# One projection of q and k per group and 32-row feature products in an attention and expert kernel

## The chip, the cores and the metric

The kernel runs on one core of one Trainium2 chip. The core has a matrix engine (TensorE, PE in the profile; PEld is its loading of weights), a vector engine (VectorE, DVE), a scalar engine (ScalarE, ACT), a general engine (GpSimd, POOL) and a queue that issues transfers (SyncE, SP). The engines run side by side, each in the order of its own program, and meet only at semaphores. SBUF is the working memory with 128 partitions, PSUM the memory of eight banks into which TensorE writes. The metric is the device time of one execution in microseconds (us); lower is better.

## The reference, cut to what matters

```
h   = layernorm(x) * (1 + ca) + sa               # x: (4, 1024, 128)
q, k, v = split(h @ w_qkv.T, 3)                  # 8 heads of 16, blocks of 32 tokens
qp  = elu(einsum('bhcsd,hdf->bhcsf', q, proj)) + 1.0     # 128 features
kp  = elu(einsum('bhcsd,hdf->bhcsf', k, proj)) + 1.0
kv  = einsum('bhcsf,bhcsd->bhcfd', kp, v)
num = einsum('bhcsf,bhcfd->bhcsd', qp, kv)
z   = 1.0 / (einsum('bhcsf,bhcf->bhcs', qp, kp.sum(axis=3)) + 1e-08)
x   = x + ga * ((num * z) @ w_out.T + b_out)
h   = layernorm(x) * (1 + cb) + sb
x   = x + gb * expert_ffn(h)                     # one of 8 experts per token, 128 -> 512 -> 128
```

elu(y) + 1 is y + 1 for positive y and exp(y) for the rest.

## The kernel before, in words

The 4096 tokens are 32 tiles of 128. Four tiles are a group, so there are 8 groups, and each group is worked through in 8 head steps (`step(g, ...)` on each engine, with `for h in range(H)` in it). After the last group come the expert slots: tokens are written to a table in device memory sorted by expert, and 39 tiles of 128 rows are read back, multiplied by the weights of their expert and written out. This tail is not touched by the change.

One head step needs the features of q and of k. The weights of projection and features are multiplied together once at the start (`fold`, L755, into `mix_hi` and `mix_lo`, split in two parts so that products in the rounded float32 form keep their precision), and `feats(g, h)` (L810 to L812) makes for each of q and k (index `j`) three products of 128x128 weights with 512 columns of the normalised, transposed input `hT`, which is also split (`hT_hi` by DVE at L1074, `hT_lo` by POOL at L424). They land in two banks, `x_ps[h % 2]`; there are two such pairs. ACT takes relu(-y) of both banks (L577) and then exp of its negative in two halves (L581); DVE makes max(y, 0) plus that, in two halves (`features`, L1179), into `phi`. TensorE then multiplies the features within blocks of 32 tokens (`scores`, L821, 16 small products), ACT copies the result (L588), and once per four heads `apply_values` (L835) multiplies it with the values. The values stand in `vbd`, spread so that each block of 32 tokens sees its own only: DVE writes them with four masked products per group (`keep_values`, L1187).

The order on each engine is written out by hand. Per head step TensorE runs `feats(g, h)`, then for some h one block of other work, then `scores` of the head two before: `values` (L852) at h = 0, `gate` (L864) at h = 3, `project_out` (L843) at h = 5, `rank` (L870) at h = 7; `apply_values` follows at h = 0 and 2, `turn_h2` (L858) at h = 2 and `turn_xn` (L763) at h = 5, each behind the scores. A pair of banks is free for head h + 2 when DVE has made the features of head h. DVE puts the pieces of the norms, the normalising, the routing and the residual of earlier groups between its `features`.

Of the kernel before, what the change touches and what calls it, by code (L numbers as in the profile page):

```python
# [19 lines left out]
P = 128  # L20
ALU = mybir.AluOpType
ACT = mybir.ActivationFunctionType
AX = mybir.AxisListType
F32 = mybir.dt.float32
# [4 lines left out]
EPS = 1e-5  # L29


def adaln_kernel(nc, x, w_qkv, w_out, b_out, proj, w_red, wg, w1, b1_t, w2, b2, c_cols, wmod, out):
# [37 lines left out]
    with ctx:  # L70
# [9 lines left out]
        proj_bd = sb("proj_bd", [P, H, FEAT])  # L80
        mix_hi = sb("mix_hi", [P, 2, H, FEAT], F32R)
        mix_lo = sb("mix_lo", [P, 2, H, FEAT], F32R)
# [10 lines left out]
        silu_bc = sb("silu_bc", [P, B, P])  # L93
# [16 lines left out]
        blk_mask = sb("blk_mask", [P, NC, VW])  # L110
# [10 lines left out]
        zeros = sb("zeros", [P, 4 * D])  # L121
# [4 lines left out]
        hT_hi = sb("hT_hi", [P, 2, GT], F32R)  # L126
        hT_lo = sb("hT_lo", [P, 2, GT], F32R)
        vals = sb("vals", [P, TG, H, HD])
# [3 lines left out]
        vbd = sb("vbd", [P, TG, H, NC, VW])  # L132
        den = sb("den", [P, TG * NC])
        rden = sb("rden", [P, TG * NC])
        o_sb = sb("o_sb", [P, TG * NC, 2, HD])
        oT = sb("oT", [P, TG, P])
# [79 lines left out]
        w_slot.append(proj_bd[:, :, :].rearrange("p h f -> p (h f)")[:, 0:F + D])  # L216
# [3 lines left out]
        yo_early = vbd[:, :, :, :, :].rearrange("p t h c w -> p (t h c w)")[:, 0:EARLY * D].rearrange("p (s d) -> p s d", d=D)  # L220
# [22 lines left out]


        l_attn = sem("l_attn"); l_mod = sem("l_mod"); l_c = sem("l_c"); l_gate = sem("l_gate"); l_x0 = sem("l_x0"); l_x = sem("l_x")
        l_exp = sem("l_exp")
        c_pool = sem("c_pool"); c_tri = sem("c_tri"); c_dve = sem("c_dve"); c_exp = sem("c_exp"); set_silu = sem("set_silu")
        p_mix = sem("p_mix"); p_cols = sem("p_cols"); p_wv = sem("p_wv"); p_rows = sem("p_rows"); p_turn = sem("p_turn"); p_gate = sem("p_gate")
        set_khi = sem("set_khi"); set_mix = sem("set_mix"); set_cols = sem("set_cols"); set_wv = sem("set_wv"); set_rows = sem("set_rows")
# [5 lines left out]
        s_neg = sem("s_neg"); s_xb = sem("s_xb"); s_gbs = sem("s_gbs"); s_scat = [sem(f"s_scat{i}") for i in range(RECS)]  # L255
        s_phi = sem("s_phi"); s_ln1 = sem("s_ln1"); s_xn = sem("s_xn"); s_vbd = sem("s_vbd"); s_nrm = sem("s_nrm")
# [12 lines left out]
        def _(sp):  # L269
            sp.dma_start(wqkv_sb[:, :, :], w_qkv.rearrange("(j r) d -> r j d", j=3)).then_inc(l_attn, 16)  # L270
            sp.dma_start(proj_bd[:, 0, :], proj.rearrange("h k f -> (h k) f")).then_inc(l_attn, 16)
            xt = xf.rearrange("(t p) d -> p t d", p=P)
            sp.dma_start(x_all[:, 0:TG, :], xt[:, 0:TG, :]).then_inc(l_x0, 16)
            sp.dma_start(cT[:, :], c_cols).then_inc(l_c, 16)
            sp.dma_start(wmod_sb[:, :], wmod).then_inc(l_mod, 16)
            sp.dma_start(wo_sb[:, :], w_out).then_inc(l_gate, 16)
# [3 lines left out]
            sp.dma_start(x_all[:, TG:NT, :], xt[:, TG:NT, :]).then_inc(l_x, 16)  # L280
            by_expert = w1b2[:, :].rearrange("p (e f) -> p e f", e=E)
            sp.dma_start(by_expert[:, :, 0:F], w1.rearrange("e d f -> d e f")).then_inc(l_exp, 16)
            sp.dma_start(w2_sb[:, :].rearrange("p (e c d) -> p e c d", e=E, c=FC),
                         w2.rearrange("e (c p) d -> p e c d", p=P)).then_inc(l_exp, 16)
            sp.dma_start(b1_cols[:, :], b1_t).then_inc(l_exp, 16)
            sp.dma_start(by_expert[:, :, F:F + D], b2.rearrange("(a e) f -> a e f", a=1).partition_broadcast(P)).then_inc(l_exp, 16)

            sp.wait_ge(c_dve, 1)
            for e in range(E + 1):
                sp.dma_start(sorted_rows[e * REGION:e * REGION + P, :], pad_rec[:, :]).then_inc(s_tail, 16)  # L290
# [1357 lines left out]
```

## Time and profile before

| | us |
|---|---|
| median of 3 runs | 293.17 |
| lowest, highest | 292.45, 293.57 |
| span of the profiled execution | 292.5 |
| TensorE busy | 264.7 |
| VectorE busy | 233.8 |
| ScalarE busy | 224.2 |
| GpSimd busy | 166.2 |

The span has three parts: the start up to the first feature product at 11.87 us, the eight groups up to 185.5 us, and the expert tail. All groups from the third to the seventh have the same length within 0.2 us, so one of them stands for five. A busy share of TensorE is not a measure of what it has left, because products overlap; the distance between the starts of two products is. For a chain of engines that wait for each other one looks at what ends last before each product.

### The profile page before, as it was taken

What the parts mean: (1) busy time and instruction counts of PE and PEld (TensorE: products, weight loads), DVE (VectorE), ACT (ScalarE), POOL (GpSimd) and SP (SyncE); (2) the same over time, 40 slices, a digit from 0 to 9 for tenths busy, and PEclk for the clock granted to TensorE, in tenths of its full rate; (3) what the DMA queues carried; (4) which work ended last, traced back from release to release, by engine and by line L of the source; (5) the groups of instructions that cost most, each with busy time, mean ns of one, the idle gap of its engine ahead of it and who ended that gap; (6) DMA issues with size and microseconds to landing.
All of it is one profiled execution on the core that took longest, in us unless ns stands there. A gap on an engine that the chain in (4) does not pass through costs nothing.

```text
span 292.5 us, 11379 instructions
## 1 busy us (share of the span) xinstructions
PE 264.7 (91%) x3952; PEld 212.3 (73%) x3953; DVE 233.8 (80%) x772; ACT 224.2 (77%) x516; POOL 166.2 (57%) x193
## 2 busy tenths in 40 slices
PE   8999799999999999999999999899686999999970
PEld 2566576678778777777777776678575999999960
DVE  3787969989999999999999989988884476676750
ACT  2589698999989989989989988856964667676740
POOL 7004154344476675675685681878788874454551
PEclk9999999999999999999999999999999999999996
DMA  5999800000001001001001011513355344444400
GB/s 149 286 358 300 199 3 2 2 4 4 2 29 56 30 29 56 31 29 57 29 29 56 29 45 70 163 58 113 126 168 176 117 126 123 112 126 131 117 28 0
DMA packets 16239, 26.13 MB, mean 89 GB/s; under 512 B 2608, under 2 KB 11060, under 8 KB 16193
## 3 DMA queue, kind: packets, MB, share of 16 engines
q1 hardware_dynamic: 12896, 17.10, 21.2%
q0 software_dynamic: 3296, 8.41, 8.0%
q8 instruction: 30, 0.49, 0.8%
q14 instruction: 17, 0.13, 0.2%
HBM read 15.32 MB, written 10.64 MB: 89 GB/s over the span
## 4 chain that ended last, share of the span: by engine, by line
PE 45%; DVE 20%; issue 8%; ACT 8%; POOL 5%; DMA 2%; POOLq 1%; ACTq 0%; DVEq 0%; SPq 0%
PE ps L885 9%; DVE phi L1179 8%; PE ps L913 8%; PE ps L810 6%; PE ps L812 4%; PE ps L811 4%; PE ps L821 3%; ACT ebuf L577 3%; ACT ebuf L581 2%; PE ps L843 2%; POOL sorted_rows L458 2%; DVE h L1248 2%; PE ps L835 2%; DVE ln_st L1231 2%; PE ps L879 1%
## 5 line engine op out<-in xcount | busy, mean ns | idle before, releaser
L1179 DVE SCALAR_TENSOR_TENSOR phi<-ps,ebuf 128x512 f32<-128x512 f32 x128 | 81.9, 680 | 13.2 <-ACT ebuf L581 13.1
L577 ACT ACTIVATE ebuf<-ps 128x1024 f32<-128x1024 f32 x64 | 65.5, 1024 | 15.5 <-PE ps L812 15.0
L581 ACT ACTIVATE ebuf<-ebuf 128x512 f32<-128x512 f32 x128 | 74.4, 636 | 0.1
L810 PE MATMUL ps<-hT_hi,mix_lo 128*128 128x512 f32 x128 | 58.4, 456 | 8.1 <-DVE phi L1179 4.5
L635 ACT ACTIVATE gT<-ps,b_cols 128x128 f32<-128x128 f32 x156 | 44.6, 367 | 17.1 <-PE ps L885 14.6
L812 PE MATMUL ps<-hT_hi,mix_hi 128*128 128x512 f32 x128 | 50.6, 396 | 0.0
L811 PE MATMUL ps<-hT_lo,mix_hi 128*128 128x512 f32 x128 | 50.6, 395 | 0.0
L913 PE MATMUL ps<-w_sb,gT 128*128 x312 | 42.3, 278 | 4.0 <-DVE y L1501 2.8
L913 PEld LDWEIGHTS ps<-w_sb,gT 128*128 128x128 f32 x312 | 37.9, 192 | 6.0 <-issue 5.9
L527 POOL DMA_INDIRECT out<-yo,tok x27 | 27.0, 1001 | 23.8 <-DVE yo L1517 21.9
L458 POOL DMA_INDIRECT sorted_rows<-rec,pos x32 | 32.6, 1017 | 8.4 <-issue 6.6
L810 PEld LDWEIGHTS ps<-hT_hi,mix_lo 128*128 128x128 f32 x128 | 24.0, 187 | 17.1 <-DVE phi L1179 6.2
L821 PEld LDWEIGHTS ps<-phi 128*32 128x32 f32 x2048 | 22.2, 112 | 15.7 <-issue 11.7
L377 POOL TENSOR_TENSOR ln_rs<-ln_ve,neg_half 128x4 f32<-128x4 f32 x16 | 16.7, 1045 | 26.6 <-DVE ln_ve L1067 23.7
L821 PE MATMUL ps<-phi 128*32 128x32 f32 x2048 | 29.3, 199 | 0.0
L812 PEld LDWEIGHTS ps<-hT_hi,mix_hi 128*128 128x128 f32 x128 | 24.0, 188 | 5.8
L424 POOL TENSOR_TENSOR hT_lo<-hT,hT_hi 128x512 fp32r<-128x512 f32 x7 | 8.9, 1277 | 34.0 <-DVE hT_hi L1074 34.0
L811 PEld LDWEIGHTS ps<-hT_lo,mix_hi 128*128 128x128 f32 x128 | 24.1, 189 | 3.7 <-issue 1.0
L885 PE MATMUL ps<-sT,x_all 128*128 128x128 f32 x184 | 25.0, 279 | 0.3 <-ACT sT L626 0.3
L885 PEld LDWEIGHTS ps<-sT,x_all 128*128 128x128 f32 x184 | 22.3, 191 | 0.8 <-issue 0.4
L588 ACT COPY a_sb<-ps 128x128 f32<-128x128 f32 x64 | 16.9, 265 | 5.0 <-PE ps L821 5.0
L1488 DVE COPY x_all<-w1b 128x640 f32 x19 | 9.8, 516 | 10.4 <-issue 10.4
(208 smaller groups left out, 465.2 us busy)
## 6 DMA issues: line engine op xcount, KB each, us to landing
rin<-sorted_rows SPq DMA_DIRECT2D x39, 192.5 KB, 2.5
w1b<-in_L_ffn_w SPq DMA_DIRECT2D x1, 2048.0 KB, 14.2
sorted_rows<-pad_rec SPq DMA_DIRECT2D x9, 192.5 KB, 6.2
w1b<-in_L_ffn_b SPq DMA_DIRECT2D x1, 512.0 KB, 7.4
sorted_rows<-rec,pos POOLq DMA_INDIRECT x32, 3.1
out<-yo,tok POOLq DMA_INDIRECT x27
wmod_sb<-in_L_wmod SPq DMA_DIRECT2D x1, 384.0 KB, 4.0
x_all<-in_L_attn_x SPq DMA_DIRECT2D x1, 256.0 KB, 3.4
```

The costliest lines, as they stand in the source:

```text
L458: g_.indirect_dma_start(out=sorted_rows[:, :], out_offset=bass.IndirectOffsetOnAxis(ap=pos[:, g % RECS, t:t + 1], axis=0), in_=rec[:, g % ...
L527: g_.indirect_dma_start(out=of[:, :], out_offset=bass.IndirectOffsetOnAxis(ap=tok[:, b:b + 1], axis=0), in_=yo[:, b, :], in_offset=None, b ...
L577: nc.scalar.activation(ebuf[:, h % 2, :, :], x_ps[h % 2], ACT.Relu, scale=-1.0).then_inc(s_neg, 1)
L581: nc.scalar.activation(ebuf[:, h % 2, j, :], ebuf[:, h % 2, j, :], ACT.Exp, scale=-1.0).then_inc(s_exp, 1)
L635: last = nc.scalar.activation(gT[:, b, c_, :], h_ps[b][:, j, i * P:(i + 1) * P], ACT.Gelu, bias=b1_cols[:, bass.ds(e * FC + c_, 1)])
L810: mm(x_ps[h % 2][:, j, :], mix_lo[:, j, h, :], hi, start=True, stop=False)
L811: mm(x_ps[h % 2][:, j, :], mix_hi[:, j, h, :], lo, start=False, stop=False)
L812: mm(x_ps[h % 2][:, j, :], mix_hi[:, j, h, :], hi, start=False, stop=True).then_inc(s_x, 1)
L821: last = mm(a_ps[c_ * BLK:(c_ + 1) * BLK, t * BLK:(t + 1) * BLK], phi[:, h % 4, 1, at:at + BLK], phi[:, h % 4, 0, at:at + BLK], start=True ...
L885: last = mm(h_ps[b % 2][:, j, i * P:(i + 1) * P], w[:, c_ * P:(c_ + 1) * P], sT[:, b % 2, :], start=True, stop=True)
L913: last = mm(y_bank(early, b), gT[:, b % 2, c_, :], w2_sb[:, bass.ds(e * (FC * D) + c_ * D, D)], start=(c_ == 0), stop=(c_ == FC - 1))
L1179: v.scalar_tensor_tensor(out=phi[:, h % 4, j, :], in0=x_ps[h % 2][:, j, :], scalar=0.0, in1=ebuf[:, h % 2, j, :], op0=ALU.max, op1=ALU.add ...
```

## The change

Projection of q and k. The fold is gone. Once a group, `project(g, j)` multiplies the 128x128 weights `wqkT` of q and of k (plain float32) with 512 columns of `hT`. ACT copies the result to `qk` in the rounded form (`keep_hi`), DVE subtracts that from the product to get the second part (`split_lo`). This is done a group ahead: `turn_xn(g + 1)` at h = 0, `project` at h = 1 and h = 4, `values(g + 1)` at h = 7. `hT_hi`, `hT_lo` and their instructions on DVE and POOL are gone.

Features. A head's feature product now contracts over 32 rows: `proj_w` holds the feature weights of two heads in each 32 rows, with the rows of the other head zero. q uses the rows of group h // 2, k the rows two groups further, so that the two lie in different quarters of the array's rows. There are three products for each of q and k, in turns of q and k, and then one more for each, of a constant `unit` with a broadcast of itself, which adds one (scaled). Everything is scaled by `SHRINK`, 2 to the power of -39.

Clamp. ACT makes one exp of both banks, straight from PSUM. DVE makes min(exp, SHRINK) and the max of that with the product, for both banks in one instruction. `keep_a` undoes the scale.

Values. ACT writes the values with a column of ones in `vals`, and SP copies them with four transfers per group to the diagonal of `vbd`, which is zeroed once. The masked products on DVE and the mask are gone.

Besides: the additions of epsilon behind both norms' moments go from DVE to POOL; the first norm runs two groups ahead; x is loaded first; loads of the expert weights are spread over groups 1 to 4 instead of standing at the start; the feature weights are loaded by ACT's queue and built on POOL (`make_proj`); the index tables are made later.

```
-            def fold(j, i):
-                mm(ps[:, 2 * i + j, :], wqkv_sb[:, j, :], proj_bd[:, 4 * i:4 * i + 4, :].rearrange("p h f -> p (h f)"),
-                   start=True, stop=True).then_inc(p_mix, 1)
+            def project(g, j):
+                if j == 0:
+                    pe.wait_ge(s_ht, g + 1)
+                elif g:
+                    pe.wait_ge(s_lo, 2 * g + 1)
+                if g == 0:
+                    pe.wait_ge(set_w, 1)
+                mm(k_first if g == 0 and j == 1 else t_ps, wqkT[:, j, :], hT[:, :], start=True, stop=True).then_inc(s_qk, 1)
...
             def feats(g, h):
                 if h == 0:
-                    pe.wait_ge(s_lo, g + 1)
...
+                    pe.wait_ge(s_lo, 2 * g + 2)
...
+                if not (g == 0 and h < 2):
+                    pe.wait_ge(s_phi, H * g + h - 1)
+                at = (h // 2 * BLK, (h // 2 + 2) % NC * BLK)
+                for w_part, part in ((0, 1), (1, 0), (0, 0)):
+                    for j in range(2):
+                        rows = slice(at[j], at[j] + BLK)
+                        mm(x_ps[h % 2][:, j, :], proj_w[rows, w_part, j, h % 2, :], qk_of(g, part, j)[rows, :],
+                           start=w_part < part, stop=False)
                 for j in range(2):
-                    if not (isinstance(g, int) and g == 0 and h < 2):
-                        pe.wait_ge(s_phi, 2 * (H * g + h) - 3 + j)
-
-                    mm(x_ps[h % 2][:, j, :], mix_lo[:, j, h, :], hi, start=True, stop=False)
-                    mm(x_ps[h % 2][:, j, :], mix_hi[:, j, h, :], lo, start=False, stop=False)
-                    mm(x_ps[h % 2][:, j, :], mix_hi[:, j, h, :], hi, start=False, stop=True).then_inc(s_x, 1)
+                    rows = slice(at[j], at[j] + BLK)
+                    last = mm(x_ps[h % 2][:, j, :], unit[rows, :], unit[rows, 0:1].broadcast_to([BLK, GT]), start=False, stop=True)
+                last.then_inc(s_x, 1)
...
-                nc.scalar.activation(ebuf[:, h % 2, :, :], x_ps[h % 2], ACT.Relu, scale=-1.0).then_inc(s_neg, 1)
-                between()
-                act.wait_ge(s_neg, H * g + h + 1)
-                for j in range(2):
-                    nc.scalar.activation(ebuf[:, h % 2, j, :], ebuf[:, h % 2, j, :], ACT.Exp, scale=-1.0).then_inc(s_exp, 1)
+                nc.scalar.activation(ebuf[:, h % 2, :, :], x_ps[h % 2], ACT.Exp, scale=1.0 / SHRINK,
+                                     bias=math.log(SHRINK) - 1.0).then_inc(s_exp, 1)
+
+            def keep_hi(g, j):
+                act.wait_ge(s_qk, 2 * g + j + 1)
+                from_ps = k_first if isinstance(g, int) and g == 0 and j == 1 else t_ps
+                nc.scalar.copy(qk_of(g, 0, j), from_ps).then_inc(s_hi, 1)
...
-                for j in range(2):
-                    dve.wait_ge(s_exp, 2 * (H * g + h) + j + 1)
-                    v.scalar_tensor_tensor(out=phi[:, h % 4, j, :], in0=x_ps[h % 2][:, j, :], scalar=0.0,
-                                           in1=ebuf[:, h % 2, j, :], op0=ALU.max, op1=ALU.add).then_inc(s_phi, 1)
-
-            def keep_values(g, c, first):
-                dve.wait_ge(s_vs, g + 1)
...
-                last = v.tensor_scalar(vbd[:, :, :, c, 0:HD].rearrange("p t h d -> p (t h) d"),
...
+                dve.wait_ge(s_exp, H * g + h + 1)
+                v.scalar_tensor_tensor(out=phi[:, h % 4, :, :], in0=ebuf[:, h % 2, :, :], scalar=SHRINK,
+                                       in1=x_ps[h % 2], op0=ALU.min, op1=ALU.max).then_inc(s_phi, 1)
...
+            def split_lo(g, j):
+                dve.wait_ge(s_hi, 2 * g + j + 1)
+                from_ps = k_first if g == 0 and j == 1 else t_ps
+                v.tensor_tensor(qk_of(g, 1, j), from_ps, qk_of(g, 0, j).bitcast(F32), ALU.subtract).then_inc(s_lo, 1)
...
+            def spread_values(g):
+                sp.wait_ge(s_vs, g + 1)
+                if g == 0:
+                    sp.wait_ge(c_vbd, 2)
+                else:
+                    sp.wait_ge(s_av, 2 * g)
+                for c in range(NC):
+                    sp.dma_start(vbd[c * BLK:(c + 1) * BLK, c, :],
+                                 vals[c * BLK:(c + 1) * BLK, :, :, :].rearrange("p t h w -> p (t h w)")).then_inc(s_vbd, 16)
```

TensorE in a middle group, around the border to the next group. Before: the last products of head 0, then the values, the scores of an earlier head and the first half of the apply.

```order
L810 MATMUL ps<-hT_hi,mix_lo 128x512
L811 MATMUL ps<-hT_lo,mix_hi 128x512
L812 MATMUL ps<-hT_hi,mix_hi 128x512
L852 MATMUL ps<-wvT,hT 128x128 x4
L821 MATMUL ps<-phi 32x32 x16
L835 MATMUL ps<-vbd,a_sb 32x68 x16
L810 MATMUL ps<-hT_hi,mix_lo 128x512
```

After, from the values of the next group to the scores behind the projection (`qk,proj_w` and `unit` are the feature products, `hT,wqkT` the projection).

```order
L905 MATMUL ps<-wvT,hT 128x128 x4
L862 MATMUL ps<-qk,proj_w 128x512 x6
L866 MATMUL ps<-unit 128x512 x2
L815 MATMUL ps<-ident,xn 128x128 x4
L876 MATMUL ps<-phi 32x32 x16
L890 MATMUL ps<-vbd,a_sb 32x68 x16
L862 MATMUL ps<-qk,proj_w 128x512 x6
L866 MATMUL ps<-unit 128x512 x2
L826 MATMUL ps<-hT,wqkT 128x512
L876 MATMUL ps<-phi 32x32 x16
```

The values have moved ahead of head 0, the transpose of xn from h = 5 to h = 0, and the projection stands between a head's feature products and the scores.

VectorE in a middle group, heads 2 to 5. Before, with the masked products L1187 and the rounding L1074:

```order
L1219 STREAM_TRANSPOSE oT<-o_sb 128x512
L1179 SCALAR_TENSOR_TENSOR phi<-ps,ebuf 128x512 x2
L1187 TENSOR_SCALAR vbd<-vals,blk_mask 128x32x16 x2
L1179 SCALAR_TENSOR_TENSOR phi<-ps,ebuf 128x512 x2
L1266 TENSOR_REDUCE top<-lg_sb 128x4
L1187 TENSOR_SCALAR vbd<-vals,blk_mask 128x32x16
L1271 TENSOR_TENSOR lgd<-lg_sb,top 128x32
L1187 TENSOR_SCALAR vbd<-vals,blk_mask 128x32x16
L1276 SCALAR_TENSOR_TENSOR cand<-lgd,rev 128x32
```

After, heads 1 to 4; `qk<-ps,qk` is `split_lo`, here of q (that of k stands behind head 5):

```order
L1230 SCALAR_TENSOR_TENSOR phi<-ebuf,ps 128x1024 x2
L1134 TENSOR_TENSOR qk<-ps,qk 128x512
L1238 TENSOR_SCALAR den<-ps 128x16
L1127 BN_AGGR ln_mv<-ln_st 128x2 x4
L1242 RECIPROCAL rden<-den 128x16
L1246 TENSOR_TENSOR o_sb<-ps,rden 128x16x16
L1254 STREAM_TRANSPOSE oT<-o_sb 128x512
L1230 SCALAR_TENSOR_TENSOR phi<-ebuf,ps 128x1024 x2
L1300 TENSOR_REDUCE top<-lg_sb 128x4
```

Four masked products and the small epsilon instruction are gone between the features, and the split stands at head 2 in front of the normalising.

## Rows read from the trace of the kernel before

**Rows 1.** The page: the chain that ended last, by engine.

```profile
PE 45%; DVE 20%; issue 8%; ACT 8%; POOL 5%; DMA 2%; POOLq 1%; ACTq 0%; DVEq 0%; SPq 0%
```

**Rows 2.** Busy time by stretch; third, fifth and last group; columns in the first line.

```profile
core 0: us, PE busy (x) PEld busy (x) DVE busy (x) ACT busy (x) POOL busy (x), PEclk, DMA share, GB/s
55.46:77.10 21.64, 21.18 (x406) 16.50 (x407) 19.24 (x59) 19.74 (x40) 8.95 (x8) 1.00 0.01 3
...
98.54:120.17 21.63, 20.92 (x406) 16.37 (x406) 20.12 (x64) 19.60 (x38) 14.36 (x14) 1.00 0.11 39
...
163.38:185.50 22.12, 20.57 (x401) 15.88 (x402) 20.58 (x66) 18.92 (x37) 12.52 (x14) 1.00 0.16 55
```

**Rows 3.** TensorE in order of time, one head: start, us, engine, line, idle before.

```profile
89.79 0.40 PE L812 MATMUL ps<-hT_hi,mix_hi 128*128 128x512 f32 x1
90.12 0.46 PE L821 MATMUL ps<-phi 128*32 128x32 f32 x32
90.51 0.50 PE L810 MATMUL ps<-hT_hi,mix_lo 128*128 128x512 f32 x1
90.84 0.40 PE L811 MATMUL ps<-hT_lo,mix_hi 128*128 128x512 f32 x1
91.07 0.40 PE L812 MATMUL ps<-hT_hi,mix_hi 128*128 128x512 f32 x1
...
91.78 0.40 PE L812 MATMUL ps<-hT_hi,mix_hi 128*128 128x512 f32 x1
92.01 1.05 PE L843 MATMUL ps<-wo_g,oT 128*128 128x128 f32 x8
```

**Rows 4.** TensorE in order of time, values, scores, apply, next head.

```profile
100.04 1.05 PE L852 MATMUL ps<-wvT,hT 128*128 128x128 f32 x8
...
101.30 0.70 PE L835 MATMUL ps<-vbd,a_sb 128*32 128x68 f32 x32
...
101.93 0.49 PE L810 MATMUL ps<-hT_hi,mix_lo 128*128 128x512 f32 x1
...
102.04 0.19 PEld L811 LDWEIGHTS ps<-hT_lo,mix_hi 128*128 128x128 f32 x1
...
102.26 0.40 PE L811 MATMUL ps<-hT_lo,mix_hi 128*128 128x512 f32 x1
```

**Rows 5.** In order of time at the start: weight loads of a plain float32 product.

```profile
7.19 0.19 PEld L755 LDWEIGHTS ps<-proj_bd,wqkv_sb 128*128 128x128 f32 x1 [0.51 <-issue]
...
7.62 0.19 PEld L755 LDWEIGHTS ps<-proj_bd,wqkv_sb 128*128 128x128 f32 x1 [0.24 <-issue]
```

**Rows 6.** Groups by line, 76.95 to 98.54 us: busy, mean ns, idle before and releaser.

```profile
L1179 DVE SCALAR_TENSOR_TENSOR phi<-ps,ebuf 128x512 f32<-128x512 f32 x17 | 10.9, 679 | 1.2 <-ACT ebuf L581 1.2
L1187 DVE TENSOR_SCALAR vbd<-vals,blk_mask 128x512 f32<-128x512 f32 x4 | 2.4, 627 | 0.0
...
L1241 DVE TENSOR_SCALAR ln_ve<-ln_mv 128x4 f32<-128x4 f32 x1 | 0.8, 799 | 0.0
...
L581 ACT ACTIVATE ebuf<-ebuf 128x512 f32<-128x512 f32 x16 | 9.3, 636 | 0.0
L577 ACT ACTIVATE ebuf<-ps 128x1024 f32<-128x1024 f32 x9 | 9.2, 1024 | 1.4 <-PE ps L812 1.3
```

**Rows 7.** VectorE in order of time, one head's features and what follows.

```profile
81.82 1.27 DVE L1179 SCALAR_TENSOR_TENSOR phi<-ps,ebuf 128x512 f32<-128x512 f32 x2
83.02 0.16 DVE L1203 TENSOR_SCALAR den<-ps 128x16 f32<-128x16 f32 x1
```

**Rows 8.** Start, in order of time: hT, its rounding, its second part, first product.

```profile
9.85 0.78 ACT L597 ACTIVATE hT<-ps,modT 128x512 f32<-128x512 f32 x1 [0.59 <-PE ps L763]
10.66 0.43 DVE L1074 CAST hT_hi<-hT 128x512 fp32r<-128x512 f32 x1 [0.21 <-ACT hT L597]
11.13 0.69 DVE L1106 TENSOR_TENSOR hT_lo<-hT,hT_hi 128x512 fp32r<-128x512 f32 x1
11.87 0.50 PE L810 MATMUL ps<-hT_hi,mix_lo 128*128 128x512 f32 x1 [0.23 <-DVE hT_lo L1106]
```

More of the change, by code:

```diff
@@ L513, in _ @@
             step(2, nxt=True, prev=True, prev2=True, firstp2=True)
-            for g in range(3, NG - 1):
-                step(g, nxt=True, prev=True, prev2=True, prev3=True)
-            step(NG - 1, prev=True, prev2=True, prev3=True)
+            for g in range(3, NG):
+                step(g, nxt=g + 2 < NG, prev=True, prev2=True, prev3=True)
             def put_early(s):
@@ L745, in keep_busy, with turn_xn @@
                     mm(bank, ones_b[:, :], ones_b[:, :].unsqueeze(1).broadcast_to([P, 4, P]), start=True, stop=True)
-            pe.wait_ge(c_pool, 2)
+            pe.wait_ge(c_ones, 1)
             keep_busy(11, m_ps)
-            pe.wait_ge(c_pool, 10)
-            pe.wait_ge(l_attn, 32)
-            def fold(j, i):
-                mm(ps[:, 2 * i + j, :], wqkv_sb[:, j, :], proj_bd[:, 4 * i:4 * i + 4, :].rearrange("p h f -> p (h f)"),
-                   start=True, stop=True).then_inc(p_mix, 1)
-            def turn_xn(g, first):
+            pe.wait_ge(c_ident, 2)
+            pe.wait_ge(l_attn, 16)
+            for j in range(3):
+                last = nc.tensor.transpose(ps[:, j, 0:P], wqkv_sb[:, j, :], ident[:, :])
+            last.then_inc(p_w, 1)
+            pe.wait_ge(set_silu, 1)
+            pe.wait_ge(l_mod, 16)
+            for j in range(2):
+                last = mm(ps[:, 3, 8 * j:8 * j + B], wmod_sb[:, j * D:(j + 1) * D], siluT[:, :], start=True, stop=True)
+            last.then_inc(p_cols, 1)
+            def turn_xn(g):
                 pe.wait_ge(s_xn, g + 1)
-                if not first:
+                if g:
                     pe.wait_ge(s_vs, g)
@@ L796, in setup_gate @@
             def setup_gate():
                 pe.wait_ge(set_turn, 1)
-                mm(ps[:, 6, 0:E], wredT[:, :], wgT[:, :], start=True, stop=True).then_inc(p_gate, 1)
+                mm(m_ps[:, 0:E], wredT[:, :], wgT[:, :], start=True, stop=True).then_inc(p_gate, 1)
             def feats(g, h):
                 if h == 0:
-                    pe.wait_ge(s_lo, g + 1)
-                if isinstance(g, int) and g == 0 and h < 2:
-                    pe.wait_ge(set_mix, h + 1)
-                hi, lo = (part[:, bass.ds(g % 2, 1), :].rearrange("p a n -> p (a n)") for part in (hT_hi, hT_lo))
@@ L831, in apply_values @@
                     pe.wait_ge(s_on, 2 * g + half)
-                to = o_ps_last if is_last(g) and half == 1 else o_ps
+                to = o_of(g, half)
                 for t in range(TG):
@@ L961, in step @@
                         apply_values(g - 1, 1, False)
-                    if h == 5 and nxt:
-                        turn_xn(g + 1, False)
-            step(0, False, False, True)
-            step(1, True, False, True)
-            for g in range(2, NG - 1):
-                step(g, True, True, True)
-            step(NG - 1, True, True, False)
+                    if h == 7 and nxt:
+                        values(g + 1)
+            turn_xn(0)
+            project(0, 0)
+            project(0, 1)
+            values(0)
+            for g in range(NG):
+                step(g, g >= 1, g >= 2, g + 1 < NG)
             pe.wait_ge(s_vs, NG)
@@ L1474, in step @@
                         if prev2:
[L1475 to L1482 removed]
+                            position_out(g - 2)
+            for g in range(NG):
+                step(g, g >= 1, g >= 2, g + 1 < NG, g + 2 < NG, firstp=g == 1, firstp2=g == 2)
             def take_weights(s, b):
```

456 lines of the change are left out of this document (225 added, 231 removed).

## The prediction

> **What bounds the kernel now.** I read the chain first: TensorE holds 45% of it and VectorE 20% [rows 1]. Then the busy time by stretch: in a middle group of 21.63 us TensorE is busy 20.92, VectorE 20.12 and ScalarE 19.60, all at a granted clock of 1.00, that is the 2.4 GHz level [rows 2]. Three engines are nearly full, so the distances between starts must tell which one sets the length. In one head the scores start 0.39 us ahead of the next head's feature products, and these take from 90.51 to 92.01 when a full-width block follows, that is 1.50 us for six [rows 3]. Inside, one product follows the other after 0.23 us (90.84 to 91.07), but the step into the feature products is 0.33 (90.51 to 90.84) and the step from their last product to the scores is 0.33 as well (89.79 to 90.12): 0.10 us more wherever TensorE changes between full and quarter-width tiles [rows 3]. So a head costs 1.60 + 0.39 = 1.99 us, eight of them 15.9 us, and the rest of the 21.6 is mostly the blocks of 128x128 products (the values alone, eight passes, about 1.0 [rows 4]). TensorE has hardly any slack; any engine that is relieved beside it gives nothing by itself.
>
> **The change part by part, for a middle group.** I keep p for the time that one pair of new feature products (q and k) takes on TensorE.
>
> Feature products: six of 0.235 us and two changes of 0.10 are replaced by four pairs and the same two changes. If q and k run side by side in their different rows, p is 0.235, the duration of one. If they don't, p is 0.47. The trace of before has no product of 32 rows. The nearest row is the apply, with tiles that differ in columns: 32 products of 68 columns between 101.30 and 101.93, 0.020 us each [rows 4], where a plain float32 pass over 512 columns takes 0.43 us [rows 5], so 68 columns would take 0.057 us one after the other. 2.9 of four tiles run at once there. With two tiles I take full overlap, p = 0.235, and keep 0.47 as the other end. A head then costs 4 x 0.235 + 0.19 = 1.13 us in place of 1.60; 8 x 0.47 = 3.8 us saved.
>
> The Trainium skill, in TensorEngine Tiling (Key Properties), says the same: tiles work independently and can load weights and multiply in parallel. TensorE: Matmul & The Clock Gate (Measured speedup vs the span model) gives 3.07 times for four row tiles; an estimate from that page's figure would put two tiles between 1.5 and 2 times, p = 0.235 to 0.31.
>
> Projection: two plain float32 products of 512 columns, two passes each. Their weight loads stand 0.43 us apart [rows 5], so 4 x 0.43 = 1.7 us added.
>
> Tile changes: feature products were full width, so nothing was lost when values, gate, output projection or rank followed directly (91.78 to 92.01 is 0.23 [rows 3]). Now each block of full-width work next to them costs one change more: the transpose of xn, two projections, gate, output projection, rank and values, 7 x 0.10 = 0.7 us. TensorEngine Tiling (Key Properties) speaks against the change here: it says that switching the tiling mode drains TensorE. By that rule, the trace agrees, and the 0.10 us is the price; without it the sum would be 0.7 us a group better.
>
> The group in total is 21.6 - 12.8 + 8 x (4p + 0.19) + 2.4 = 12.7 + 32p. At p = 0.235 this is 20.2 us, a gain of 1.3 to 1.4; it is zero at p = 0.278. The margin is thin: 0.04 us a pair.
>
> ScalarE: the two exps (16 in 9.3 us) go, relu becomes exp on the same 1024 elements (1.02 us [rows 6]), and two copies of 512 columns come, about 0.6 each by the size of the exp rows. 19.6 - 9.3 + 1.2 = 11.5 us: far from the bound.
>
> VectorE: four masked products (2.4 us), the epsilon instruction (0.8) and the rounding (0.43) go [rows 6, 8]; two splits of 0.69 come [rows 8]; the one 1024-wide feature instruction costs as much as the two did or a little less (81.82 to 83.02, 1.20 us [rows 7]). 20.1 - 3.6 + 1.4 - 0 to 0.5 = 17.4 to 17.9 us. That fits into 20.2 with some two us to spare. This relief is what lets TensorE have its gain; without it VectorE's 20.1 would be as late as TensorE.
>
> GpSimd loses `hT_lo` and gets two tiny additions; it is at 14.4 of 21.6 [rows 2]. Its wait for `hT_hi` stood in front of a scatter and of the next norm; now both norms start with a wait for VectorE's moments, and behind it in GpSimd's queue stand a scatter and the scale of a record, which nobody needs before the following group. Cost nothing. The values by transfer: SP waits for the apply at h = 2 of a group, the reader is the apply at h = 0 of the next, some 15 us later. Four transfers cost nothing unless the queue is held for longer than that; the loads of expert weights are issued behind them, in groups 1 to 4, with the next spread a group later, and nothing on SP is urgent until the last group. The prologue's padding writes move past the spread for group 1, hidden too.
>
> **Start.** Before, hT starts at 9.85 and the first product at 11.87 [rows 8]. x comes one issue earlier, but VectorE now scales the turned weights ahead of the modulation columns; I leave hT's end at 10.6. Then projection 0.86, copy 0.6, split 0.69, and about 0.6 more because the k half follows through the same two engines: first feature product near 13.4, +1.5 us. The ends are +0.5 (the earlier x counts fully) and +3.
>
> **Sum over the groups.** Group 0: VectorE and the modulation rows bind it; it loses the masked products and gets splits, I take -2.0 (0 to -3). Group 1 has no gate, rank or turn of h2 and waited for features more; -1.5. Groups 2 to 6: 5 x -1.3 = -6.5; the ends are -2, if new waits cost 0.9 us a group, and -10, if the tile changes cost nothing more than today. Group 7, 22.12 us [rows 2]: no projection, no transpose, no values behind it, and VectorE, at 20.58 the later engine there, loses 3.2 us; -3.0 (-1 to -4). Tail: the same instructions, 0. Sum: +1.5 - 2.0 - 1.5 - 6.5 - 3.0 = -11.5 us. 292.5 - 11.5 = 281.0 for the profiled execution; the median of before is 0.7 above its span, so 281.7 us. With all ends of the small terms the forecast's own range is 274 to 290.
>
> **Rivals.**
> 1. No overlap of q and k: p = 0.47. Against it speaks the apply; for it, that this row is of column tiles and of another form of number. It adds 32 x 0.235 = 7.5 us a group, 60 us in all: 342 us. This is the case on the other side, and it decides from p = 0.278 on.
> 2. Weight loads in the same rows wait. Head by head the next pair uses the same rows, and if a load there had to wait for the product in flight, p would be 0.235 plus a load, at most 0.13 (eight loads and passes of the values in 1.05 us [rows 4]). Against it: the load at 102.04 starts while the product of 101.93 runs over all rows, and the next product follows at 102.26 [rows 4]. It would add 32 x 0.13 = 4.2 us a group: 315 us. TensorE: Matmul & The Clock Gate (The mechanism) states that loads overlap a running product only when the row groups differ; by that rule this case would hold, and the trace disagrees for full-width loads. A milder form of 1 or 2, p near 0.3, gives 281.7 + 8 x 2.1 = 298.
> 3. The gain turns into a wait on VectorE. Features are now given and freed whole, not in halves: products 1.13, exp 1.02, features 1.2 and three hand-overs make about 3.7 us for a pair of banks, against 5.0 in two heads. That leaves 1.3 us; heads 6, 7, 0 and 2 carry most of VectorE's other work, and where a head is later than that TensorE waits. If this takes the whole gain of the middle groups: 281.7 + 6.5 = 288, up to 292.
> 4. Something not in the views (a granted clock that falls to 1.2 GHz, transfers that come late): 5%, mostly slower.
>
> **How the numbers follow.** Forecast 0.66, rival 1 0.09, rival 2 with its milder form 0.10 (half each), rival 3 0.10, rival 4 0.05. The range must leave out no more than 0.2: it starts at 273, below the forecast's own, and goes to 300 to take in rival 3 and the milder form; 315 and 342 stay out. About 0.5% (1.5 us) is what a measurement can tell from no change. Faster: nearly all of the forecast and two thirds of rival 3, 0.73. Same: the last third and a little, 0.06. Slower: 0.21.
>
> **What would show it.** Right: the starts of feature products in pairs within some ten ns, pairs 0.235 us apart; middle groups of 20.2 us; ScalarE busy near 12 us a group; no wait of the apply for `vbd`; first feature product near 13.4. Wrong: starts 0.23 us apart one by one (rival 1); pairs at 0.36 (rival 2); TensorE idle ahead of feature products and released by VectorE for over 1 us a group (rival 3).

## The result and the profile after

The changed kernel takes 305.27 us (median of 4 runs, 300.59 to 316.24), the kernel before 293.37 us in the same sitting (median of 4, 292.45 to 293.76). The ratio is 1.0295 with a 95% interval of 1.0222 to 1.0368: slower by 3%, where 281.7 us and a gain of 4% were forecast, and outside the range of 273 to 300. The ratio rests on the two faster runs, 300.59 and 303.59 us; the profiled execution took 306.96 us, with a span of 304.9 and a mean granted clock of 0.892. The four clocks are 0.911, 0.891, 0.892 and 0.845, in the order of the times: 300.59, 303.59, 306.96, 316.24.

The times follow the clocks, except that the middle two clocks are equal. The page of the profile has the granted clock in tenths, in 40 slices. Before (slices of 7.3 us):

```profile
PEclk9999999999999999999999999999999999999996
```

After (slices of 7.6 us), with the busy share of TensorE above it:

```profile
PE   7599799999999999999999989999778799999970
PEclk9689979996559999996559998799999799999996
```

TensorE stays busy and the clock falls all the same. The next view gives, for stretches of 3 us, busy time and count of each engine (PE, PEld, DVE, ACT, POOL), then the granted clock, the share of the DMA engines and GB/s:

```profile
69.00:72.00 3.00, 3.00 (x53) 2.04 (x49) 2.93 (x11) 1.38 (x3) 1.72 (x3) 0.93 0.41 93
72.00:75.00 3.00, 3.00 (x38) 1.43 (x38) 2.19 (x6) 1.35 (x3) 1.60 (x2) 0.50 0.86 271
93.00:96.00 3.00, 3.00 (x78) 1.80 (x76) 1.22 (x1) 2.29 (x4) 1.08 (x2) 1.00 0.18 68
141.00:144.00 3.00, 3.00 (x40) 1.68 (x40) 2.08 (x6) 0.87 (x3) 2.53 (x3) 0.50 0.11 42
```

A clock of 0.50 is the 1.2 GHz level. TensorE has no idle time in any of the four, and in the two slow ones it gets half as many instructions done (38 and 40 against 78). Nor is it idle ahead of a long fall: in every stretch from 54 to 180 us it is busy for 3.00 of 3.00 us, and in that time the clock falls twice, near 71.5 and near 139.8 us, for some 20 us each. Two shorter falls, near 41 and near 188 us, come close behind or in a stretch with idle time. (The ends of products are modelled in the trace, so very short gaps would not show; before_rows32, below, doesn't rest on this.) The transfers are no common sign: a share of 0.86 in one, 0.11 in the other.

Group by group, from one hT activation (L645) to another, the same view:

```profile
62.87:90.61 27.74, 27.74 (x426) 18.62 (x420) 19.05 (x53) 13.15 (x23) 11.70 (x14) 0.66 0.27 72
90.61:111.21 20.60, 20.60 (x445) 14.28 (x437) 16.55 (x47) 13.06 (x23) 10.98 (x13) 0.97 0.35 106
111.21:131.01 19.80, 19.80 (x435) 13.63 (x425) 17.77 (x52) 13.07 (x24) 13.55 (x16) 1.00 0.35 110
131.01:158.80 27.79, 27.79 (x431) 18.80 (x425) 19.49 (x56) 13.15 (x24) 16.61 (x19) 0.66 0.13 40
```

The group at a clock of 1.00 takes 19.80 us, where a middle group of before took 21.6 [rows 2] and 20.2 were forecast. The two groups at 0.66 take 27.7 and 27.8 us, each 7.9 to 8.0 more than the undisturbed one. So the change does in TensorE's program what the sum said, and the clock takes it back.

One head of the undisturbed group, and one at half clock (start, duration, engine, line; TensorE alone):

```profile
111.29 0.97 PE L862 MATMUL ps<-qk,proj_w 32*128 32x512 f32 x6
112.10 0.38 PE L866 MATMUL ps<-unit 32*128 32x512 f32 x2
112.41 1.13 PE L826 MATMUL ps<-hT,wqkT 128*128 128x512 f32 x2
```

```profile
81.72 1.64 PE L862 MATMUL ps<-qk,proj_w 32*128 32x512 f32 x6
83.17 0.62 PE L866 MATMUL ps<-unit 32*128 32x512 f32 x2
83.72 0.21 PE L923 MATMUL ps<-pick,before 128*128 128x40 bf16 x1
```

At the full clock eight products stand in 111.29 to 112.41, 1.12 us; before, six took 1.50 without the second change of tiles [rows 3]. At half clock they take 81.72 to 83.72, 2.00 us.

ScalarE and VectorE in the undisturbed group (engine, operation, count, busy time and mean ns, then the idle time before them and what ended it), to set beside [rows 6, 7]:

```profile
L622 ACT ACTIVATE ebuf<-ps 128x1024 f32<-128x1024 f32 x8 | 8.2, 1026 | 4.3 <-PE ps L866 4.3
L1230 DVE SCALAR_TENSOR_TENSOR phi<-ebuf,ps 128x1024 f32<-128x1024 f32 x8 | 9.7, 1209 | 1.8 <-ACT ebuf L622 1.8
L1134 DVE TENSOR_TENSOR qk<-ps,qk 128x512 fp32r<-128x512 f32 x2 | 1.4, 684 | 0.0
```

What idle time they have goes back to TensorE: ScalarE waits for its products, VectorE for ScalarE.

The start has a second miss. The rows that answer to [rows 8]:

```profile
7.29 1.03 POOL L437 TENSOR_TENSOR stage<-stage,half_mask 128x512 f32<-128x512 f32 x1
7.33 3.34 DVE L1148 TENSOR_SCALAR xn<-x_all,ln_mv,ln_rs 128x128 f32<-128x128 f32 x4
9.07 1.26 POOL L442 TENSOR_TENSOR proj_w<-stage,proj_w 128x512 fp32r<-128x512 f32 x1
10.73 1.12 PE L815 MATMUL ps<-ident,xn 128*128 128x128 f32 x4 [2.36 <-DVE xn L1148]
11.88 0.78 ACT L645 ACTIVATE hT<-ps,modT 128x512 f32<-128x512 f32 x1 [5.13 <-PE ps L815]
12.71 3.78 PE L826 MATMUL ps<-hT,wqkT 128*128 128x512 f32 x4 [0.87 <-ACT hT L645]
17.90 0.50 PE L862 MATMUL ps<-qk,proj_w 32*128 32x512 f32 x2 [0.20 <-DVE qk L1134]
```

The first feature product starts at 17.90, forecast 13.4, before 11.87. VectorE's four xn instructions take 3.34 us while GpSimd builds the feature weights (before, 1.11), and the projection of q and k takes 3.78 us at a granted clock of 0.50.

### The profile page after: what moved, and what is told of

The parts are those of the page before. It is cut to its first block, busy times and chain, and to the rows that moved or that the text cites. A ratio compares the mean times of both kernels' runs of the same rounds, so it can differ in the third digit from the quotient of the medians.

```text
span 304.9 us, 11533 instructions
## 1 busy us (share of the span) xinstructions
PE 277.7 (91%) x4106; PEld 207.1 (68%) x4107; DVE 217.8 (71%) x668; ACT 168.6 (55%) x400; POOL 160.7 (53%) x201
## 4 chain that ended last, share of the span: by engine, by line
PE 65%; DVE 8%; issue 5%; POOL 5%; DMA 2%; ACT 1%; POOLq 0%; DVEq 0%; SPq 0%
PE ps L862 17%; PE ps L938 9%; PE ps L966 8%; PE ps L876 7%; PE ps L826 4%; PE ps L866 4%; PE ps L898 3%; PE ps L905 3%; DVE phi L1230 3%; PE ps L890 3%; POOL sorted_rows L509 2%; PE ps L917 2%; PE ps L815 2%; DMA sorted_rows<-rec,pos 2%; PE ps L932 1%
## 5 line engine op out<-in xcount | busy, mean ns | idle before, releaser
L1230 DVE SCALAR_TENSOR_TENSOR phi<-ebuf,ps 128x1024 f32<-128x1024 f32 x64 | 77.5, 1211 | 36.0 <-ACT ebuf L622 36.0
L862 PE MATMUL ps<-qk,proj_w 32*128 32x512 f32 x384 | 69.5, 470 | 3.4 <-DVE phi L1230 3.2
L862 PEld LDWEIGHTS ps<-qk,proj_w 32*128 32x128 f32 x384 | 35.1, 208 | 15.1 <-DVE phi L1230 3.9
L876 PEld LDWEIGHTS ps<-phi 128*32 128x32 f32 x2048 | 24.6, 120 | 24.2 <-issue 16.2
L574 POOL DMA_INDIRECT out<-yo,tok x27 | 27.1, 1003 | 25.1 <-DVE yo L1538 24.4
L876 PE MATMUL ps<-phi 128*32 128x32 f32 x2048 | 32.1, 208 | 0.2 <-issue 0.2
L636 ACT ACTIVATE a_sb<-ps 128x128 f32<-128x128 f32 x64 | 17.6, 275 | 21.5 <-PE ps L876 21.5
L866 PE MATMUL ps<-unit 32*128 32x512 f32 x128 | 26.8, 415 | 0.0
L826 PE MATMUL ps<-hT,wqkT 128*128 128x512 f32 x32 | 21.4, 764 | 0.9 <-ACT hT L645 0.9
L866 PEld LDWEIGHTS ps<-unit 32*128 32x128 f32 x128 | 13.4, 205 | 3.6
L676 ACT COPY sT<-ps 128x128 f32<-128x128 f32 x39 | 10.4, 266 | 8.9 <-PE ps L932 7.7
```

The lines of the kernel that those rows point to most:

```text
L574: g_.indirect_dma_start(out=of[:, :], out_offset=bass.IndirectOffsetOnAxis(ap=tok[:, b:b + 1], axis=0), in_=yo[:, b, :], in_offset=None, b ...
L636: nc.scalar.activation(a_sb[:, h // HH, h % HH, :, :], a_ps.rearrange("p (t s) -> p t s", t=TG), ACT.Copy, scale=SHRINK ** -2).then_inc(s_ ...
L826: mm(k_first if g == 0 and j == 1 else t_ps, wqkT[:, j, :], hT[:, :], start=True, stop=True).then_inc(s_qk, 1)
L862: mm(x_ps[h % 2][:, j, :], proj_w[rows, w_part, j, h % 2, :], qk_of(g, part, j)[rows, :], start=w_part < part, stop=False)
L866: last = mm(x_ps[h % 2][:, j, :], unit[rows, :], unit[rows, 0:1].broadcast_to([BLK, GT]), start=False, stop=True)
L876: last = mm(a_ps[c_ * BLK:(c_ + 1) * BLK, t * BLK:(t + 1) * BLK], phi[:, h % 4, 1, at:at + BLK], phi[:, h % 4, 0, at:at + BLK], start=True ...
```

## The experiments

The theory after the result: **rows at work**. The granted clock falls because the products of the features use 32 + 32 of the array's 128 rows at a time, though TensorE is never idle. The rivals: idle time and waits of TensorE, the bursts of transfers, or the other parts of the change (the shorter ScalarE and VectorE work, the values by transfer).

**rows64: the same program with 64 rows in each product.** q uses one half of the rows and k the other, in the same eight weight loads and eight products a head. In the six products with `proj_w` the weights of the other three heads in those rows are zero, so that the rows with weights that are not zero are as few as in the changed kernel; the two with `unit` have 64 such rows in place of 32.

```
-                at = (h // 2 * BLK, (h // 2 + 2) % NC * BLK)
+                at = (h // 4 * 64, (1 - h // 4) * 64)
...
-                        rows = slice(at[j], at[j] + BLK)
-                        mm(x_ps[h % 2][:, j, :], proj_w[rows, w_part, j, h % 2, :], qk_of(g, part, j)[rows, :],
+                        rows = slice(at[j], at[j] + 64)
+                        mm(x_ps[h % 2][:, j, :], proj_w[rows, w_part, j, h % 4, :], qk_of(g, part, j)[rows, :],
```

> The changed kernel with one thing altered: q and k feature products contract over 64 rows each (q in one half of the array's rows, k in the other), with the weight rows of the other heads zero, in place of 32. Same number of instructions and columns, the full computation. Theory A (the granted clock falls because the 32-row products keep too few of the array's rows at work): the clock stays at 0.97 or above, middle groups of about 20 us, 279 to 285 us. Theory B (the clock falls because of the order and the waits of the new program, whatever the rows): clock near 0.89 as in the changed kernel, 299 to 307 us.

Measured: 290.06 us (287.11 to 291.87, 4 runs, clocks 0.962 to 0.968), ratio to before 0.9855 (0.979 to 0.992). Two groups of it, and its row of the clock:

```profile
63.85:83.75 19.90, 19.90 (x435) 13.73 (x425) 17.27 (x48) 13.07 (x24) 9.04 (x11) 1.00 0.38 105
103.56:123.36 19.80, 19.80 (x435) 13.66 (x425) 17.77 (x52) 13.06 (x24) 13.58 (x16) 1.00 0.36 110
PEclk9669999999999999999999999999998899999996
```

The first of these is the group that took 27.74 us at 0.66 in the changed kernel; the second has the same 19.8 us, 435 products, load of transfers and relief of ScalarE as the undisturbed group there, and the clock is 1.00 in both. All that differs in the groups is how many rows a product uses. That takes out the rivals for the groups, and turns 305 into 290 us, 1.5% below before. Rows whose weights are zero count here as rows in use, in six of the eight products. Nor is it the chip: on one and the same chip proj_late, the changed kernel with one wait more, has a clock of 0.902 and rows64_late 0.976 to 0.981 (both below).

The time itself was missed: 279 to 285 us were expected by this theory, 299 to 307 by its rival, and 290 lies between. The first feature product comes at 20.25 us in place of 17.90, because GpSimd has twice as many weights to build; the clock is low there as well. The runs for the start, below, take this up.

**rows128: all 128 rows for each product**, so that q and k can't run side by side. Each product then contracts over all rows with the same weights, and so mixes four heads: the selection of the head is left out.

```
-                at = (h // 2 * BLK, (h // 2 + 2) % NC * BLK)
+                at = (0, 0)
...
-                        rows = slice(at[j], at[j] + BLK)
+                        rows = slice(0, P)
```

> The changed kernel with feature products over all 128 rows for q and for k (it sums over all heads, so the features are not those of the reference). A pair can no longer run side by side: both theories expect pairs at 0.47 us in place of 0.235, groups of about 27.5 us and 330 to 342 us if the clock is whole. Theory A: granted clock 0.98 or above in the groups. Theory B: it still falls in some groups, below 0.93, and the time is over 345.

Measured: 327.99 us (2 runs, clocks 0.968 and 0.981), ratio 1.1197 (1.1169 to 1.1226), just below the 330 to 342 us expected.

```profile
96.81:122.67 25.86, 25.86 (x435) 20.01 (x425) 18.08 (x50) 12.94 (x25) 14.00 (x16) 1.00 0.28 84
100.15 1.67 PE L862 MATMUL ps<-qk,proj_w 128*128 128x512 f32 x6
101.66 0.60 PE L866 MATMUL ps<-unit 128*128 128x512 f32 x2
102.19 0.46 PE L876 MATMUL ps<-phi 128*32 128x32 f32 x32
```

Eight products now need 100.15 to 102.19, 2.04 us, in place of 1.12. A group is 6.06 us longer. So q and k do run side by side in the changed kernel, and what that is worth is 6 us a group; rival 1's price was about right (7.5 us, less 0.7 for the seven tile changes that this kernel doesn't have), its condition false. A group of 27.5 us was expected and is 25.86; the clock in it is 1.00, as the theory says.

**before_rows32: the kernel before, with its feature products over the first 32 rows only** (the other 96 rows of the contraction are left out). Nothing of the change is in it.

```
-                    mm(x_ps[h % 2][:, j, :], mix_lo[:, j, h, :], hi, start=True, stop=False)
+                    mm(x_ps[h % 2][:, j, :], mix_lo[0:32, j, h, :], hi[0:32, :], start=True, stop=False)
...
```

> The kernel before, its order and its waits untouched, with the three feature products of each of q and k contracting over the first 32 rows only (part of the contraction is left out). A product takes as long whatever its rows. Theory A: the granted clock falls below 0.95 in the groups and the time rises to 298 or more. Theory B: clock 0.99 and 293 us as before.

Measured: 400.28 us (398.71 to 404.49, clocks 0.659 to 0.671), ratio 1.3647 (1.3589 to 1.3706).

```profile
134.00:171.60 37.60, 37.60 (x407) 27.22 (x407) 20.00 (x63) 19.95 (x37) 14.31 (x14) 0.50 0.06 23
PEclk9995655555555555555555555555589998999997
```

The theory expected a clock below 0.95 and 298 us or more. A group of 21.6 us becomes one of 37.6 by using fewer rows in the same products. TensorE is busy in all of it. This is the strongest run of the study: a kernel that had the full clock in all groups loses it with no other edit.

**before_rows64 and before_rows96** repeat it with 64 and 96 rows (the other 64 or 32 rows are left out); the slices read `[0:64]` and `[0:96]`.

> The kernel before with the three feature products of q and of k contracting over the first 64 rows only (part of the contraction is left out), order and waits untouched. Before: clock 0.99, 293 us; the same with 32 rows: clock 0.66, 400 us. Theory A in its strict form (what counts is the number of rows at work at a time, so that one product of 64 rows is like a pair of 32): clock between, falling in part of the groups, 0.85 to 0.95 and 298 to 325 us. If only tiles of 32 rows are at fault: clock 0.99 and 293 us.

> The kernel before with its feature products over the first 96 rows in place of 128 (rows 96 to 127 of the contraction are left out; instructions, columns and order are the same). Theory (the granted clock goes by how many rows of the array are at work): between the whole clock of before (0.99, 293 us) and that of 64 rows (0.83 and 0.73, 339 and 378 us); with a steep edge it may be whole: clock 0.93 to 0.99, 293 to 312 us. Rival (anything less than the full 128 rows loses it): clock at or under 0.83, 339 us or more.

Measured: with 64 rows 338.62 and 377.83 us, at clocks of 0.828 and 0.726; with 96 rows 294.32 us (292.05 to 296.3, clocks 0.971 to 0.987), ratio 1.0059 (1.0001 to 1.0117).

```profile
PEclk9999795557555555599977999969998999999996
80.00:100.00 20.00, 20.00 (x211) 14.15 (x210) 11.90 (x34) 11.66 (x23) 5.46 (x6) 0.53 0.01 2
```

These lines are of the kernel with 64 rows. In that with 96 only two slices are below 9, apart from the last, which is 6 before too:

```profile
PEclk9999889999999999999999999999999999999996
```

With 96 rows the run is as expected (0.93 to 0.99, 293 to 312 us). With 64 rows both runs lie outside what was expected (0.85 to 0.95, 298 to 325 us), and they differ by 39 us, so neither is the figure for 64 rows; the faster one, at 338.62, is far above before all the same. So the clock rises with the rows in this kernel: 0.66, 0.73 and 0.83, 0.97 to 0.99. It is also not a matter of 32-row products alone. The changed kernel has 64 rows at work too and a clock of 0.89, between 64 and 96 rows here. It has them for a smaller part of the time (1.1 of 2.5 us a head, where before_rows64 has 1.5 of 2.7 [rows 3]); that this makes the difference isn't shown.

**busy1: more work of full width.** One bf16 product of 128 rows and 512 columns goes ahead of each head's features, into a bank that the features overwrite.

```
+                if True:
+                    keep_busy(1, x_ps[h % 2][:, 0, :])
```

> The changed kernel plus one bf16 product of 128 rows and 512 columns ahead of each head's feature products, into the bank that these overwrite (64 in all, about 0.235 us each at the 2.4 GHz level, 15 us). Theory A: the granted clock stays at 0.97 or above, and 281.7 + 15 = 295 to 299 us. Theory B: clock near 0.89 and 312 us or more.

Measured: 304.88 us (300.62 to 305.83, clocks 0.953 to 0.969), ratio 1.0324 (1.025 to 1.0398). The clock rises from 0.89 to 0.96, and the time stays. By the theory it would have been 0.97 or above and 295 to 299 us, by the rival near 0.89 and 312 or more; it is neither. 64 products, about 15 us by the estimate of 0.235 us each, cost about as much as they give back, and the clock still falls in places:

```profile
72.00:90.00 18.00, 18.00 (x305) 11.36 (x307) 13.20 (x35) 9.18 (x18) 5.36 (x8) 0.91 0.40 106
PEclk9599969999799799799999999999999999999996
```

The direction speaks for the theory, the size was missed. Filling is no substitute for using the rows.

**proj_late: the changed kernel, with GpSimd's weight building behind xn.** This is about the start alone.

```
+                pool.wait_ge(s_xn, 1)
                 g_.tensor_tensor(proj_own[:, :, :, :], proj_raw[:, :, :].unsqueeze(2).broadcast_to([P, 2, 2, FEAT]),
```

> The changed kernel with one wait added: GpSimd builds the feature weights behind the first normalised input xn instead of beside it. In the changed kernel VectorE's four xn instructions took 3.34 us beside GpSimd's three, against 1.11 before. Theory C (VectorE is held while GpSimd works on SBUF beside it): xn takes about 1.1 us, the transpose starts near 8.6 instead of 10.7 and the first feature product is 1.5 to 2.5 us earlier than 17.90. Theory D (xn is long for another reason, x comes late or the epsilon on GpSimd): xn stays above 3 us.

Measured: 302.68 us (1 run, clock 0.902). One run says nothing on the time, because the clock alone moves it by more; the rows of the start are what it is read for.

```profile
7.26 1.11 DVE L1149 TENSOR_SCALAR xn<-x_all,ln_mv,ln_rs 128x128 f32<-128x128 f32 x4 [0.61 <-POOL ln_rs L401]
10.11 3.53 PE L827 MATMUL ps<-hT,wqkT 128*128 128x512 f32 x4 [1.03 <-ACT hT L646]
15.04 0.50 PE L863 MATMUL ps<-qk,proj_w 32*128 32x512 f32 x2 [0.30 <-DVE qk L1135]
```

xn takes 1.11 us again instead of 3.34, and the first feature product comes 2.9 us earlier (1.5 to 2.5 were expected). In rows64, whose GpSimd instructions are twice as wide (1024 elements), the same xn took 5.70 us. So VectorE was held by GpSimd's work. The Trainium skill, in Perfetto Trace Analysis (Optimizing Scalar/DVE Operations), says that GpSimd and VectorE share a read port of SBUF; by that the trace agrees: 3.34 us beside GpSimd, 1.11 without. The projection is hardly shorter (3.53 us).

**rows64_late, rows64_best, rows64_order: versions.** rows64_late is rows64 with that wait, and with 2 + 4 full-width products that keep TensorE at work ahead of the turn of xn and ahead of the projection. rows64_best splits the raw feature weights first (half or a quarter of the elements), and ScalarE masks them with four instructions. rows64_order moves the split behind xn, and gives each mask its own semaphore step, so that a head waits for its own weights only.

```
+            for e in range(4):
+                last = nc.scalar.activation(proj_w[:, :, :, e, :], proj_s[:, :, :, :].bitcast(F32), ACT.Copy,
+                                            scale=half_mask[:, e:e + 1])
...
             turn_xn(0)
+            keep_busy(4, m_ps)
             project(0, 0)
```

> The 64-row kernel, with the feature weights built behind xn and six bf16 products of 128 rows put into the idle time of TensorE in the first 10 us. The 64-row kernel had its first feature product at 20.25 us, with xn taking 5.70 us and the granted clock at half from 9 to 19 us. Theory C with a whole clock: xn 1.1 us, first feature product near 14.5 (bound by the building of the weights, 5.3 us behind xn), and 290.1 - 5.5 = 284 to 286 us. Without effect of either: 290.

> As rows64_late, but the weights are split in two parts on GpSimd before the norm (256 columns twice) and masked by four ScalarE instructions of 512 columns, which has nothing to do until 11.9 us. Nothing is on GpSimd beside xn. First feature product at 13 to 13.5 us, that is 7 us earlier than in the 64-row kernel: 282 to 284.5 us. If VectorE's and TensorE's own chain is longer than thought: as rows64_late, 284 to 286.

> Kernel rows64_best with another order at the start alone: GpSimd splits the raw feature weights behind VectorE's first xn, and ScalarE makes the four masked weight sets one by one (the first behind hT, the others behind the two copies of q and k), so that heads 1, 2 and 3 wait for their own set only. Theory (VectorE is held beside GpSimd's weight building, and ln_rs was late in rows64_best): xn 7.3 to 8.4 with about 1.1 us, hT near 9.6, projection near 10.4, first feature product near 14 in place of 16.0 in rows64_best; the groups stay 19.8 us at a granted clock of 1.00; time 282.5 us (281 to 284.5) where rows64_best had 284.4. Rival: xn of the next group, which GpSimd makes behind the split, comes later and takes the gain back, as in rows64_late: time 284.4 or more with the first feature product all the same near 14.

| kernel | first feature product | us (lowest to highest) | ratio to before |
|---|---|---|---|
| rows64 | 20.25 | 290.06 (287.11 to 291.87) | 0.9855 (0.979 to 0.992) |
| rows64_late | 14.15 | 287.86 (286.95 to 289.05) | 0.9779 (0.9723 to 0.9835) |
| rows64_best | 16.02 | 284.44 (282.45 to 286.15) | 0.9681 (0.9632 to 0.9731) |
| rows64_order | 13.80 | 283.77 (281.90 to 286.14) | 0.9677 (0.9631 to 0.9724) |

Against what was expected: rows64_late has its first feature product where it should be (14.5), but not its time (284 to 286). rows64_best has its time (282 to 284.5), but not its first product (13 to 13.5): there GpSimd's splits hold up its own piece of the norm, and xn starts at 8.59 us in place of 7.3. rows64_order has both (near 14; 281 to 284.5).

rows64_late shows that an early start isn't all: GpSimd then makes the second group's xn later, and TensorE waits for it.

```profile
19.14 0.66 PE L817 MATMUL ps<-ident,xn 128*128 128x128 f32 x4 [3.81 <-POOL xn L430]
```

In rows64_order that wait is gone (0.4 us), and with the clock kept up the projection takes 1.98 us:

```profile
8.54 0.62 PE L823 MATMUL ps<-ident,xn 128*128 128x128 f32 x4
10.19 1.98 PE L834 MATMUL ps<-hT,wqkT 128*128 128x512 f32 x4 [0.16 <-ACT hT L646]
13.80 0.97 PE L871 MATMUL ps<-qk,proj_w 64*128 64x512 f32 x6
```

Its groups run 1.9 us earlier than those of rows64_best (the last hT starts at 137.10 against 139.00), yet the medians differ by 0.7 us and the ratios not at all, less than a measurement can tell. In the one traced execution of each, the clock from 157 us to 250 us is 0.95 to 0.97 in rows64_order and 1.00 in rows64_best over the same part of its program; but the first is the slowest of its four runs and the second the fastest of its six, so this doesn't explain the medians. Where the earlier start goes is open. Both versions beat the kernel before by 3% and the changed kernel by 6% (ratio 0.968 against 1.0295).

## Why the prediction was wrong

**The step that failed** is the one that has no number in the sum: the granted clock was taken over from before. "All at a granted clock of 1.00" was read in [rows 2], and every duration of the sum, 0.235 us a product, was then used at that clock, for a program whose largest block of products uses half of the rows. The case stood under rival 4 with 5% and no price. Two groups at 0.66 cost 27.74 + 27.79 - 2 x 20.2 = 15.1 us of the 304.9 - 281.0 = 23.9 us by which the span is over the forecast. The trace of before could not have told it: all its products of note run over all 128 rows, the scores and the apply too (they are narrow in columns), and its granted clock was whole in every group. What could have been done is to see that no row of before supports the old clock for a new kind of product, and to give the case a price. The trace after has that price: eight products 2.00 us against 1.12, a group at 0.66 27.7 us against 19.8. A rival with that price would stand at 297 us with two such groups and at 312 with four (7.5 us each on top of 281.7), and the range of 273 to 300 would have had to be wider.

The Trainium skill, in TensorE: Matmul & The Clock Gate (HAM oscillation), puts a fall of the clock down to gaps in which TensorE is idle. By that rule this kernel would keep its clock from 54 to 180 us, where the trace has no such gap; the clock falls twice. The measurement decides, and it says that how many rows of the array are at work counts too.

**The start** was mis-sized: +1.5 forecast, ends +0.5 and +3, measured 17.90 - 11.87 = +6.0. hT was left at 10.6 and starts at 11.88, ends at 12.66: VectorE's xn is 2.2 us longer beside GpSimd, which no row of before had shown. And the projection stood in the sum as 0.86 for one; it took 3.78 for both, at a clock of 0.50 from 12 to 15 us, behind 5 us (7 to 12) in which TensorE was busy for 1.7. In rows64_order, where full-width products fill that idle time, it takes 1.98. Together 4.5 of the 23.9 us. Of the other 4.3, the comparison with rows64 shows 1.4 us between the second and the fourth hT (20.04 to 62.87 against 22.39 to 63.85), where the clock falls again, and 1.4 behind the last one. The rest isn't traced.

**What was right**, read where the clock was whole:
- p, the disputed number: 0.24 us a pair (111.86 to 112.10 for one). rows128 shows the other end, 2.04 us for eight products where four pairs take 1.12. Rival 1's condition is false.
- Weight loads in the same rows don't wait (rival 2): at p = 0.365 the group would be 24.4 us; it is 19.8.
- The group: 12.7 + 32p = 20.2, measured 19.80 in the changed kernel and 19.80 to 19.90 in the middle groups of rows64. The 0.4 us are within the ends given for the tile changes.
- VectorE: 17.4 to 17.9 forecast, 17.77 measured. All feature products of the execution together waited 3.2 us for it (rival 3).
- ScalarE: 11.5 forecast, 13.07 measured. The term took 9.3 us of durations off a busy time in which instructions overlap; it is far from the bound and cost nothing.
- The values by transfer: no product of the apply waited for `vbd`.
- The whole sum comes out near, though in part by luck. rows64_best and rows64_order have the same groups at the full clock, and take 284.44 and 283.77 us, beside the forecast of 281.7. Part by part in the traces, from the first feature product to the end of VectorE's last feature instruction: 177.3 us before (11.87 to 189.14), 161.0 in rows64_best (16.02 to 177.04) and 161.4 in rows64_order (13.80 to 175.16), so the groups give 16 us where 13.0 were forecast (the five middle ones 9.1 in place of 6.5). The start takes back 4.2 us in rows64_best (1.5 forecast) and 1.9 in rows64_order, and the rest of the program, put at 0, is 103.4 us before, 103.5 in rows64_best and 108.7 in rows64_order. Two misses cancel.

The ends of the terms were added up a little wrong as well: they give 275 to 292 us, not 274 to 290. It changes nothing.

So the overlap was right and its gain real, 1.8 us a group. It was paid for with rows, and the price of rows wasn't in the sum.

**What stays open**: why the clock of the changed kernel falls in some groups and not in others of the same program, and why one more full-width product a head (busy1) doesn't hold it. The runs give how often it falls, not when. Whether rows with zero weights would count if the data passing over them were zero too was not run either.

## What to carry to other kernels

When a change packs small products side by side, count the rows that are in use at once, and look at the granted clock of the changed kernel before anything else: TensorE that is busy in every microsecond can still be at 1.2 GHz. If half of the rows would be idle, use them with zero weights; here that cost no time in the groups (19.8 us either way) and kept the clock there. The wider weights have to be built, though: in rows64 that put the first feature product 2.35 us later, until the start was rearranged. And keep GpSimd's wide instructions out of the stretch in which VectorE is on the path.

## What the runs showed of the hardware

- The mean granted clock of an execution by the rows of the feature products: 32 rows 0.66 (0.50 in the group shown), 64 rows 0.73 and 0.83, 96 rows 0.97 to 0.99, 128 rows 0.99 (before_rows32, 64, 96 and before); 32 + 32 side by side 0.85 to 0.91, 64 + 64 side by side 0.96 to 0.97 with a low clock only at the start and in two slices of the tail.
- Two products in different quarters of the rows run fully side by side: 0.24 us for two (changed kernel), as for one over all rows (rows128, eight in 2.04).
- The clock falls in a stretch in which TensorE is never idle: busy from 54 to 180 us, 0.50 for 20 us twice (changed kernel).
- Rows with zero weights count for the clock, with data passing over them that is not zero: 1.00 in the group that had 0.66 (rows64).
- Four 128x128 scalings of VectorE take 1.11 us alone (before, proj_late), 3.34 beside GpSimd instructions of 512 elements (changed kernel), 5.70 beside those of 1024 (rows64).
